# Softmax sums of a causal attention: one group of four 128x32 products a round, spread back over the heads by ScalarE

## The reference, cut to what matters

```python
q = (x @ Wq).reshape(B, N, H, Dh).transpose(0, 2, 1, 3)      # H = 16 heads, Dh = 64
s = jnp.einsum('bhid,bhjd->bhij', q * scale, k)
gm = jnp.max(s, axis=-1, keepdims=True)
p = jnp.where(causal_mask, 0.0, jnp.exp(s - gm))
num = jnp.einsum('bhij,bhjd->bhid', p, v)
out = num / (jnp.sum(p, axis=-1, keepdims=True) + EPS)       # the sum of this line
return out.transpose(0, 2, 1, 3).reshape(B, N, H * Dh) @ Wo + bo
```

## Time and profile before

| what | value |
|---|---|
| median of 3 executions | 1817.34 us (1815.21 to 1819.09) |
| the profiled execution, from its first to its last instruction (span) | 1813.0 us |
| the attention, up to the first product of the experts | 1260.4 us of it |
| busy: TensorE, VectorE, GpSimd, ScalarE | 96%, 78%, 72%, 55% of the span |

### The profile page before, as it was taken

One profiled execution on the slowest core, in us unless ns is written; L12 is line 12 of the kernel. 1 busy time (PEld: TensorE's weight loads), 2 busy tenths in 40 slices (PEclk: granted clock), 3 DMA queues, 4 the chain that ended last, 5 costly groups with the idle time before them and its releaser, 6 DMA issues. The chain is left out here.

```text
span 1813.0 us, 32705 instructions
## 1 busy us (share of the span) xinstructions
PE 1740.1 (96%) x11830; PEld 1270.1 (70%) x11830; DVE 1421.8 (78%) x2459; ACT 998.0 (55%) x1985; POOL 1312.4 (72%) x1353
## 2 busy tenths in 40 slices
PE   6999999999999999999999999998999969889998
PEld 4767776677777677776776767765888746568786
DVE  6778777777787777777787777875999948979887
ACT  3544444444444444535444444543899876648876
POOL 1777667676777677677776676777999957738998
PEclk9999999999999999999999999999999989989999
DMA  3000000000000000000000000001000000000000
GB/s 95 1 1 1 1 1 1 1 1 1 1 1 1 1 1 1 1 1 1 1 1 1 1 1 1 1 24 31 2 1 1 1 1 1 0 1 7 13 13 18
DMA packets 15089, 10.89 MB, mean 6 GB/s; under 512 B 433, under 2 KB 14546, under 8 KB 14930
## 3 DMA queue, kind: packets, MB, share of 16 engines
q1 hardware_dynamic: 14930, 8.80, 1.7%
HBM read 6.70 MB, written 2.10 MB: 5 GB/s over the span
## 5 line engine op out<-in xcount | busy, mean ns | idle before, releaser
L1148 DVE TENSOR_REDUCE attn_neg<-attn_shared 128x2 f32<-128x1024 f32 x512 | 611.9, 1223 | 262.6 <-PE attn_shared L1328 261.6
L1013 ACT ACTIVATE attn_prob<-attn_shared 128x1024 f32<-128x1024 f32 x288 | 295.3, 1027 | 366.7 <-PE attn_shared L1357 366.6
L915 POOL TENSOR_TENSOR attn_row_sum<-attn_row_sum,attn_prob 128x1024 f32<-128x1024 f32 (+3 forms) x256 | 418.3, 1634 | 24.5 <-POOL attn_row_sum L910 0.4
L312 ACT ACTIVATE experts_weighed<-experts_y,kept_gate 128x128 f32<-128x128 f32 x1024 | 279.5, 412 | 47.6 <-PE experts_y L559 39.7
L892 POOL TENSOR_TENSOR attn_prob<-attn_prob,attn_below 128x256 f32<-128x256 f32 x256 | 188.8, 737 | 132.7 <-ACT attn_prob L1013 132.7
L405 DVE SCALAR_TENSOR_TENSOR experts_acc<-experts_y,kept_gate,experts_acc 128x128 f32<-128x128 f32 x896 | 247.2, 343 | 22.7 <-PE experts_y L559 20.4
L910 POOL TENSOR_TENSOR attn_row_sum<-attn_prob 128x1024 f32<-128x1024 f32 x64 | 135.8, 2122 | 171.3 <-ACT attn_prob L1013 168.7
L1324 PE MATMUL attn_shared<-attn_qk_hi 64*128 64x512 f32 x1024 | 229.9, 429 | 8.4 <-DVE attn_neg L1148 4.5
L1167 DVE RECIPROCAL attn_den<-attn_den 128x256 f32<-128x256 f32 x128 | 214.7, 1719 | 0.6 <-ACT attn_den L1042 0.6
L1328 PE MATMUL attn_shared<-attn_qk_hi,attn_qk_lo 64*128 64x512 f32 x1024 | 212.7, 393 | 0.0
L1326 PE MATMUL attn_shared<-attn_qk_lo,attn_qk_hi 64*128 64x512 f32 x1024 | 211.5, 390 | 0.0
(11 more groups left out here) (260 smaller groups left out, 3326.8 us busy)
## 6 DMA issues: line engine op xcount, KB each, us to landing
kept_x<-in_L_attn_a_x_dram SPq DMA_DIRECT2D x4, 512.0 KB, 9.2
kept_half_raw<-_ffn_expert_weights_dram SPq DMA_DIRECT2D x4, 512.0 KB, 4.6
out_dram<-kept_x SPq DMA_DIRECT2D x8, 256.0 KB, 2.3
attn_prob<-in_L_attn_a_Wkv_dram SPq DMA_DIRECT2D x2, 512.0 KB, 6.8
attn_prob<-in_L_attn_a_Wq_dram SPq DMA_DIRECT2D x1, 512.0 KB, 4.6
attn_wo<-in_L_attn_a_Wo_dram SPq DMA_DIRECT2D x1, 512.0 KB, 5.6
attn_bo<-in_L_attn_a_bo_dram SPq DMA_DIRECT2D x1, 64.0 KB, 5.7
linear_weights_raw<-in_L_attn_b_Wg_dram SPq DMA_DIRECT2D x1, 64.0 KB
```

The costliest lines, as they stand in the source:

```text
L312: ins = act.activation(weighed[n][:, e, :], y[fill(pair, quad, odd) % RING][:, e * D:(e + 1) * D], ACT.Copy, scale=k.gate[:, c, quad * PER ...
L915: pool.tensor_tensor(row_sum[n][:, :, at:], row_sum[n][:, :, at:], src, ALU.add).then_inc(add_ok, 1)
L1013: act.activation(prob[n % RING][:, :, :], buffer((p, t))[:, :, :], ACT.Exp).then_inc(exp_ok, 1)
L1148: dve.tensor_reduce(neg[p % 2][:, :, b, half], buffer((p, b, half))[:, :, :], AX.X, ALU.max, negate=True).then_inc(max_ok, 1)
```

## The change

Both query halves of both heads of a pair now go through one group of four products with 32 columns of ones each. They write the four quarters of 32 partitions of the bank `alone` ("quadrants"): quadrant 2h+n holds the sums of head h and half n. The group for pair r-1 is issued in step 0 of round r; the one at the end of step 1 is gone. There is one `denominator` and one `inverse` (of two pieces) for a pair, over the 128x512 block `den[0]`.

The quotient is then wanted on all 64 partitions of its head. ScalarE's new function `spread` makes that: four copies of 32x512 from `den[0]` into `den[1]` and onto the halves that it lacks, a wait for them, and two more copies within `den[0]`. It stands behind `product_out(r, 0)` at the end of step 1. Both `normal` of a pair now run in step 0 of the round after. `row_sum[0]` and `o[0]` get a second buffer; to make room, one `qk_lo` buffer lies in the part of `w_lo` that the attention leaves free, and the last two expert weights wait until it has been read.

```diff
         if valid(r - 1):
-            single.append(("sum", r - 1, 1))
+            single.append(("sum", r - 1, 0))
         if valid(r + 1):
             single.append(("turned", r + 1, 0))
-        if valid(r):
-            single.append(("sum", r, 0))
...
-        qk_lo = [sb(f"qk_lo{i}", [P, 2, N], F32R) for i in range(2)]
+        qk_lo = [sb("qk_lo0", [P, 2, N], F32R), k.w_lo[:, 16:32, :].rearrange("p (m x) d -> p m (x d)", m=2)]
...
-        ones = sb("ones", [P, DH])
+        ones = sb("ones", [P, QUADRANT])
...
+        def quadrant(h, n):
+            return slice(QUADRANT * (2 * h + n), QUADRANT * (2 * h + n + 1))
...
                 if i in (0, 8):
-                    need(pool, sum_ok, 2 * (p - 1) + n + 1)
+                    need(pool, sum_ok, p if n else p - 1)
...
             def normal(p, n):
 
-                pool.wait_ge(inv_ok, PIECES * (2 * p + n + 1))
+                pool.wait_ge(spread_ok, p + 1)
                 pool.wait_ge(o_ok, 2 * p + n + 1)
...
                     if t == 0 and valid(r - 2):
+                        normal(r - 2, 0)
                         normal(r - 2, 1)
-                    if t == 1 and valid(r - 1):
-                        normal(r - 1, 0)
...
-            def denominator(p, n):
-                act.wait_ge(sum_ok, 2 * p + n + 1)
-                need(act, norm_ok, 2 * (p - 1) + n + 1)
-                act.activation(den[n][:, :], alone[:, :], ACT.Identity, bias=sum_eps[:, :], scale=1.0).then_inc(den_ok, 1)
+            def denominator(p):
+                act.wait_ge(sum_ok, p + 1)
+                need(act, norm_ok, 2 * p)
+                act.activation(den[0][:, :], alone[:, :], ACT.Identity, bias=sum_eps[:, :], scale=1.0).then_inc(den_ok, 1)
+
+            def spread(p):
+
+                act.wait_ge(inv_ok, PIECES * (p + 1))
+                for h in range(2):
+                    for n in range(2):
+                        act.activation(den[1][quadrant(h, n), :], den[0][quadrant(h, 1), :], ACT.Copy).then_inc(moved_ok, 1)
+                act.wait_ge(moved_ok, 4 * (p + 1))
+                for h in range(2):
+                    ins = act.activation(den[0][quadrant(h, 1), :], den[0][quadrant(h, 0), :], ACT.Copy)
+                ins.then_inc(spread_ok, 1)
...
                         if valid(r):
                             product_out(r, 0)
-                            denominator(r, 0)
+                        if valid(r - 1):
+                            spread(r - 1)
...
-                    if valid(r - 1):
+                    if t == 1 and valid(r - 1):
                         for piece in range(PIECES):
-                            inverse(r - 1, t, piece)
+                            inverse(r - 1, piece)
...
-            def sums(p, n):
-                alone_free(("sum", p, n))
-                pe.wait_ge(add_ok, ADDS * p + (11 if n else 7))
+            def sums(p):
+
+                alone_free(("sum", p, 0))
+                pe.wait_ge(add_ok, ADDS * (p + 1))
                 for h in range(2):
-                    ins = pe.matmul(alone[head(h), :], ones[:, :], row_sum[n][:, h, :], start=True, stop=True)
+                    for n in range(2):
+                        ins = pe.matmul(alone[quadrant(h, n), :], ones[:, :], row_sums(p, n)[:, h, :], start=True, stop=True)
                 ins.then_inc(sum_ok, 1)
...
                 if valid(r - 1):
-                    sums(r - 1, 1)
+                    sums(r - 1)
...
                     for i in range(3, 8):
                         product(r, i)
-                    sums(r, 0)
```

## The result

The changed kernel takes 1899.17 us (median of 4 runs, 1898.62 to 1901.11), against 1817.01 us for the kernel before in the same comparison: a ratio of 1.0451, 95% interval 1.0438 to 1.0464. It is slower, as forecast, but by 82 us and not by 34, and outside the range of 1836 to 1880.

What follows compares the result with a forecast made beforehand. The prediction took TensorE to bound the attention. Its terms, -27.5 + 2.2 + 50.7 + 8 = +33.4 us on 1817.3, gave a forecast of 1851 us, with a range of 1836 to 1880.

Steps and rivals of the forecast that it cites:

- the direction: Whole kernel: 1.8% slower than before; chances slower 90%, same 2%, faster 8%.
- an exponential that is not late: Turn of a round: the six copies pass in the slack, TensorE's saving stays whole, 1797 us; chance 8%.
- TensorE's saving: Turn of each of 32 rounds: one sums group goes, 0.86 us each, -27.5 us; passages in the middle, +2.2 us.
- not side by side: Middle sums group: the four products run two by two, 27.5 us more, 1878 us; chance 12%.
- the stall: Turn of a round: TensorE waits for the late first exponential, 30 x 1.69 = +50.7 us.
- the four copies start at 0.53, 1.06, 1.59 and 2.12: ScalarE at the turn: start times in us after the copy of `pv` starts, at a pace of 0.53.
- if copies between quarters of the partitions do not overlap at all: Bound on the copies' pace: 0.63 us in place of 0.53, the wait grows by 0.7 us, +21 us.
- the clock: Rival, in the rounds: each TensorE gap brings a low-clock stretch costing 1.5 us, 30 of them +44 us, 1895; chance 5%.
- a gap of 1.7 us in dense work should not do it: Turn of a round: TensorE's clock stays full, as in the window from 1256 to 1260 us, 2.05 of 4.00 us busy.
- The end of the attention: Last pair: `spread`, a multiplication and all 32 Wo records precede the experts, +5.4 to +8.8 us, taken as +8.

Runs made afterwards that it cites:

- the four-copy version: The changed kernel without the two last of the six copies, so a quarter of the quotients is not filled: 1840.05 us, ratio 1.0133.
- that with the first reciprocal ahead: The changed kernel with four copies ahead of the copy of `pv`, two behind, and the first reciprocal ahead of VectorE's step 1 maxima: 1811.32 us, ratio 0.9969.

## Why the prediction was wrong

**Right: the direction, the place and the mechanism.** Copies ahead of the first exponential of a round hold TensorE, once in each of 30 rounds. Taking them away gives 1799 us, where the prediction's case of an exponential that is not late gave 1797; changing their number or their place moves the time as that wait says.

**Right: TensorE's saving.** Four products side by side take what two took, so the rival "not side by side" fell. The saving is 0.71 us a round and not 0.79: 2.6 us over 32 rounds.

**Wrong in size: the stall.** I had 1.69 us and it was 2.50. The step that failed is "the four copies start at 0.53, 1.06, 1.59 and 2.12": they have a pace of 0.65, so the exponential starts 0.69 us later. I took 0.53 from the earlier trace rows, where both operations have 128 partitions and begin at the same one; the prediction named the other case, +21 us "if copies between quarters of the partitions do not overlap at all", and gave it too little weight. The remaining 0.12 us lie between the end of the exponential and the score (0.14 measured, 0.02 counted). Together 30 x 0.81 = 24 us. The Trainium skill, "ScalarE: Activation LUTs", § What ACT_TABLE_LOAD costs, says that one ScalarE operation after the other overlaps by about 93 ns; the runs agree where both begin at the same partition (0.30 us long, 0.20 apart) and not for copies of 32 partitions that follow each other at different quarters (0.63 long, 0.65 apart). With this error alone the time would have been about 1875 us, inside the range.

**Wrong: the clock, which took the time out of the range.** The step that failed is "a gap of 1.7 us in dense work should not do it". I judged it by a single window at the end of the attention and gave the rival 5%. The gap was longer than I had it, and that mattered: 1.0 us brought no low stretch in some 30 stalls, 2.3 us brought 13 in 29, 3.6 us one at each of 29. Each lost 1.56 us, about the 1.5 that I had put: 13 x 1.56 = 20 us. So the second error hangs on the first, at least in part: the rival's condition was itself a function of the term that I had mis-sized. Whether 30 stalls of 1.7 us would have lowered the clock was not measured (stalls of 2.16 us did in 4 of 15 cases, single gaps of 1.75 and 2.05 us in the four-copy version and in that with the first reciprocal ahead did not); my forecast, harmless, is neither shown nor refuted.

**The end of the attention.** +9.5 us where I had 8. The low clock there is as assumed: over the Wo records (5.82 us for 32) it is 0.59.

```profile
1330.00:1336.00 6.00, 0.00 (x0) 0.00 (x0) 4.79 (x16) 3.76 (x6) 0.66 (x1) 0.50 0.00 0
1336.00:1342.00 6.00, 5.25 (x29) 5.28 (x30) 0.00 (x0) 0.00 (x0) 2.24 (x3) 0.59 0.00 0
```

The Wo records take 3.8 us more than the 16 of before (I had counted some 4.6), and `spread` 3.9 us and not 3.4. The rest is a term that I left out: the reciprocals start 4.98 us after the sums group, and before they started 3.00 us after it. The copy of `pv` waits 2.36 us for GpSimd's two multiplications of the pair before (they now run together), and the copy of the sums stands behind it. 3.8 + 3.9 + 2.0 = 9.7.

**The sum by measured terms**: -32 x 0.71 = -22.7; stalls 30 x 2.5 = +75; clock +20; end +9.5. That gives +82, and 84.0 were measured up to the experts; the fourteenth low stretch and the last two rounds, which run differently, are not in it.

What stays open is which of the stalls of 2.3 us lowers the clock. They are alike in length and in the work around them, both kinds of round have both sorts, and 16 of 29 do not. What differs is the moment at which they fall: where a low stretch comes, it begins between 0.3 us before the end of the stall and 1.5 us behind it. That was not followed up.

## What to carry to other kernels

Work that goes onto an engine with 45% idle time can still cost most of its own length when it stands ahead of the one operation that frees the bound engine's buffer: here 3.9 us of copies a round cost 2.5 us of stall and another 0.7 us of clock, and copies in stretches where their engine waits anyway cost the rounds nothing. So look for the place before the price, and for the second engine that must be early for it (here VectorE's reciprocal). A stall of the bound engine is to be priced with what the clock does behind it, and both sizes together: a stall that comes out half as long again may change from harmless to one that brings half-rate stretches.

## What the runs showed of the hardware

- Single gaps of TensorE in otherwise dense work lower its clock some of the time: gaps of 1.0 us never (some 30), of 2.16 us 4 times in 15, of 2.3 us 13 times in 29, of 3.3 us 11 times in 15, of 3.6 us in all 29. The low stretches in the rounds were 3.4 us long at 0.50 to 0.51 of full (three of the gaps of 3.6 us and four of those of 3.3 had one of 6.8), and one of 3.4 us made a round 1.56 us longer. The Trainium skill, "TensorE: Matmul & The Clock Gate", § Why this matters for your kernels, says that idle gaps between bursts of products bring the half rate back; the traces agree, and show it for shorter gaps than the page warns of.
- ScalarE copies on 32 partitions that follow each other at different quarters do not overlap: 32x512 takes 0.63 us at a pace of 0.65, 32x256 0.415 at 0.44. On 128 partitions 128x128 takes 0.30 us at a pace of 0.20. A copy of 32x512 in the first quarter did overlap the 128x512 before it (0.49 us from start to start against 0.60 long), and one that read the second quarter did not (0.62).
- Four fp32 products of 32 columns, writing the four quarters of a bank, run side by side and take the time that two of 64 columns took: eight records of 0.59 us in 1.06 us.
- VectorE copies of 32x512 took 0.42 us while GpSimd was idle and 0.60 to 0.84 us beside its additions and masks, with the same source and destination (line 1190 at 1320.63 and in the rounds).
